# A graph, mixing and feed-forward block on one core: one reciprocal for two tiles, key sums between the qkv products, half of the weight splitting moved into layer 1

## Chip, cores, metric

The kernel runs on one core of one Trainium2 chip. The metric is the device time of one execution in microseconds. The engines are called as in the profile: PE (TensorE), DVE (the vector engine), ACT (ScalarE), POOL (GpSimd) and SP (SyncE, whose queue issues most of the transfers).

## What is computed

The reference, cut to what matters here (N = 3125 nodes, D = 256, 53125 edges with self loops and neighbours of a graph that `src` and `dst` give):

```python
xn = layernorm(x)
x  = x + gnn(xn, src, dst) + mix(xn)      # three graph layers: 256->1024->512->256
x  = x + ffn(layernorm(x))                # for the top 1561 rows by a router's score

# mix: per row, after a first scaling of xn
h   = relu(batchnorm(h @ w_qkv))                     # 768 wide: q, k, v parts
t   = proj(h);  s = proj(conv(t, w_dw, w_pw))        # second set of 768, in groups of 32
q, k, v of cat(t, s), 96 wide a group, norms clamped to a ball
vk  = v k^T over one position;  out = vk q / (sum(v) + eps)
ft  = proj(out) @ w_res + b_res;  fx = tanh(|ft|) ft / |ft|
```

With one position a row, the attention comes to `q * sum(k) * v / (v + eps)` in each group; the quotient is what the change is about. `eps` is scaled by the clamped norm of the row, so it is a tensor of its own (`veps`).

## The kernel before, in words

The work has these stages: norms, edge keys and the batch norm's statistics (up to 131 us); the mixing part (131 to 404 us); graph layer 1 (404 to 765 us), layers 2 and 3, the router's search, and the feed-forward part.

**Mixing part.** The 25 tiles of 125 rows are taken in NC = 5 chunks of 626 columns (features on the partitions). Every engine has its own loop over the chunks, and its order is written out by hand. All waits are on semaphores.

- PE (L2126 to L2158): `outs(c-1)` sums the squares of the previous chunk's four output tiles and multiplies the first two row tiles with `w_res`; `key_sums(c, n)` sums the keys within groups for each of the four tiles n (two of h, two of s) into banks 6 and 7; `outs_turned(c-1)` turns norms and does the other three row tiles; `hidden(c+1, m)` are the six qkv products of the next chunk, `spread(c+1)` its six convolution products, and `norm_spread(c+1)` broadcasts its norm sums, also into banks 6 and 7. `degrees` are in-degree counts from one-hot batches (chunks 0 and 1), `bias_product` (L1981) a product of `be1` with `w2` in chunk 2.
- DVE (L1088 to L1103): clamps the norms (`umax`, L1090), then for each tile `quotient` (L1032: an addition L1035, a reciprocal L1037, a product L1039) and `weigh` (L1042: the key product L1046 and the weighing L1048). `besides` puts one-hot batches (`half_batch`, L803), `scales`, pieces and rows between them. `rows_mixed` (L1051) reads the products with `w_res` of the previous chunk.
- ACT (L1618 to L1650): the square root that makes `veps` (L1620), evacuation and squares of the next chunk (`hidden`, `spread`), squares of the outputs (`out_square`), norms (`mixed_norms`), squares of weights, and the tables PREPARED_AT.

**Splitting for layer 1.** Layer 1's operands are float16 pairs of a high and a low part. There are twelve weight pieces (`wpieces`, L384: four of w1, eight of w2) and 25 row tiles. A piece is scaled by ACT into `wtemp` (`pieces_high`, L1517), its low part is made by DVE (`piece_low`, L1018), and ACT copies the high part back (`pieces_kept`, L1527). Rows go the same way (`rows_high`, L1532, `row_low`, L1024) through three buffers. PREPARED_AT and PIECES_AT / ROWS_AT (L445) say in which chunk, between which tiles, each is done.

**Layer 1.** For each tile PE adds up 25 count tiles times rows (`aggregate`, L2161), does half of the second product of tile t-2, turns the sums (`turn_y`), turns the normed rows of t-1 (`turn_x`), ends the second product and does the first product (`step1`, L2242). ACT begins a tile with `halve_rows` (L1680), DVE with `sum_rows` and ends it with `hidden1` (L1161). PE waits for all twelve pieces before tile 0:

```python
pe.wait_ge(sem("rows1_ready"), T)
pe.wait_ge(sem("ft_done"), T)
pe.wait_ge(sem("wpiece_done"), len(wpieces))
```

**Counts.** POOL scatters the edge counts into DRAM with 416 indirect transfers in 26 groups (L638), starting when edge indices and `evalue` (L1599) are ready, and sets a flag when a group has landed (`landing`, L632). SP fetches the counts of a tile into a ring of four; for layer 1 it waits for as many flags as the tile needs (`landed`, L514), and for the ring.

## Time and profile before

| | us |
|---|---|
| runs | 1365.85 median of 3 (1365.02 to 1368.14) |
| the profiled execution, own time | 1365.98 |
| its span in the profile | 1364.2 |
| PE busy | 1235.3 (91%) |
| DVE busy | 735.9 (54%) |
| ACT busy | 485.0 (36%) |
| POOL busy | 524.4 (38%) |
| mean granted clock of TensorE | 0.963 |

Shares of busy time are means over stages with different limits, so the stages have to be looked at one by one. Matmuls are all recorded at one helper's line (L1853); they are told apart by their tiles: `kones` are key sums, `ones` sums of squares, `wm` qkv, convolution or `w_res` products, `rows,scr` aggregations. A granted clock of 1.00 is 2.4 GHz, 0.50 is 1.2 GHz. "idle before" is the time that an engine had nothing to do just before an instruction, with what ended it.

### The profile page before, as it was taken

The numbers are of one execution on the slowest core, as the hardware profiler recorded it, in microseconds if no ns is written. First come the engines' busy times: TensorE is split into PE (matmuls) and PEld (weight loads), VectorE is DVE, ScalarE is ACT, GpSimd is POOL, SyncE is SP. The second block draws the span as 40 slices with busy tenths as digits, with TensorE's granted clock in tenths as the row PEclk, the third lists the DMA queues.
The fourth block names the chain that finished last, engine by engine and source line by source line (L and its number), as shares of the span: only waits on it lengthen the run. The fifth ranks groups of instructions, "written<-read, shape, count | busy, mean of one in ns | idle before, by whom it ended". The sixth has DMA issues, their size and how long they took to land.

```text
span 1364.2 us, 19298 instructions
## 1 busy us (share of the span) xinstructions
PE 1235.3 (91%) x6623; PEld 817.1 (60%) x6623; DVE 735.9 (54%) x1489; ACT 485.0 (36%) x1058; POOL 524.4 (38%) x551
## 2 busy tenths in 40 slices
PE   0998887897669999999999999999999999996995
PEld 0764564654445666666666566666666666663575
DVE  5674997868644555455454522322222268887244
ACT  2414674468532222232232223222122234432463
POOL 2001777777777777777701300070000000000623
PEclk9988898899879999999999999999999999998998
DMA  9880000000313222322122132212122146643201
GB/s 269 294 274 1 2 1 1 1 1 1 83 56 91 71 65 54 80 54 66 41 77 69 45 91 64 69 47 69 53 61 69 47 125 169 171 116 113 47 19 35
DMA packets 56391, 104.48 MB, mean 77 GB/s; under 512 B 25455, under 2 KB 40804, under 8 KB 56328
## 3 DMA queue, kind: packets, MB, share of 16 engines
q1 hardware_dynamic: 35800, 100.21, 25.9%
q0 software_dynamic: 20528, 3.47, 1.8%
q8 instruction: 35, 0.57, 0.2%
q14 instruction: 28, 0.23, 0.1%
HBM read 75.87 MB, written 27.67 MB: 76 GB/s over the span
## 4 chain that ended last, share of the span: by engine, by line
PE 80%; DVE 11%; ACT 4%; issue 2%; DMA 1%; SPq 0%; POOL 0%; DVEq 0%; ACTq 0%; POOLq 0%
PE psum L1853 77%; DVE scr L1037 3%; PE psum L2214 2%; DVE acc L807 1%; DMA rows<-in_x 1%; PE psum L2192 1%; DVE scr L1039 1%; DVE scr L1035 1%; DMA scr<-picked,eidx 0%; PE psum L1899 0%; PE psum L2207 0%; ACT scr L1566 0%; SPq L470 0%; DVE acc L809 0%; DVE scr L1320 0%
## 5 line engine op out<-in xcount | busy, mean ns | idle before, releaser
L642 POOL DMA_INDIRECT counts<-big,eidx x416 | 422.9, 1016 | 250.3 <-issue 130.8
L1853 PE MATMUL psum<-big,scr 125*125 125x512 f16 x1250 | 278.8, 379 | 1.0 <-DVE big L1157 1.0
L1853 PE MATMUL psum<-rows,scr 125*125 125x512 f16 x1250 | 274.7, 379 | 2.9 <-issue 1.6
L1853 PEld LDWEIGHTS psum<-rows,scr 125*125 125x125 f16 x1250 | 170.7, 137 | 102.3 <-issue 2.4
L1853 PEld LDWEIGHTS psum<-big,scr 125*125 125x125 f16 x1250 | 170.0, 137 | 94.9 <-DVE big L1157 1.5
L1853 PE MATMUL psum<-wb,scr 128*125 128x512 f16 x600 | 137.5, 379 | 1.4 <-DVE scr L1140 1.4
L1853 PEld LDWEIGHTS psum<-wb,scr 128*125 128x125 f16 x600 | 81.1, 137 | 45.8 <-DVE scr L1140 1.9
L1121 DVE TENSOR_SCALAR scr<-psum,col 125x256 f32<-125x256 f32 x25 | 12.1, 484 | 172.6 <-PE psum L1853 172.6
L1853 PE MATMUL psum<-big,wm 128*128 128x313 f32 x312 | 94.2, 453 | 8.2 <-ACT big L1556 4.6
L684 POOL DMA_INDIRECT scr<-picked,eidx x13 | 23.2, 1787 | 180.0 <-issue 180.0
L1853 PEld LDWEIGHTS psum<-big,wm 128*128 128x128 f32 x312 | 61.3, 201 | 38.7 <-issue 9.3
L1037 DVE RECIPROCAL scr<-scr 128x626 f32<-128x626 f32 x20 | 81.3, 4066 | 0.7
L1140 DVE TENSOR_TENSOR scr<-psum,scr 128x1000 f16<-128x1000 f32 x25 | 30.0, 1199 | 86.0 <-ACT scr L1697 86.0
L738 DVE BATCH_NORM_STATS2 col<-scr 125x6 f32<-125x512 f32 x75 | 49.5, 689 | 45.4 <-ACT scr L1706 28.1
L1853 PE MATMUL psum<-wa,scr 128*125 128x512 f16 x300 | 68.9, 380 | 1.0 <-DVE scr L1135 0.9
L673 POOL IOTA scr<- 125x63 f32 x1 | 0.2, 196 | 175.3 <-PE psum L1853 175.3
L1667 ACT ACTIVATE scr<-psum,col 128x125 f32<-128x125 f32 x100 | 37.3, 454 | 69.6 <-PE psum L2192 69.6
L1853 PEld LDWEIGHTS psum<-wa,scr 128*125 128x125 f16 x300 | 40.9, 137 | 24.8 <-DVE scr L1135 1.4
L664 POOL TENSOR_SCALAR scr<-wa,col 128x512 f32<-128x512 f32 x4 | 6.3, 1565 | 123.8 <-DVE col L1226 123.5
L1697 ACT CAST scr<-psum 128x1000 f16<-128x1000 f32 x25 | 24.8, 992 | 80.7 <-PE psum L1853 71.8
L807 DVE TENSOR_TENSOR acc<-acc,scr 104x2000 bf16<-104x2000 bf16 x32 | 38.2, 1194 | 19.7 <-PE psum L1853 19.5
L1853 PE MATMUL psum<-wc,scr 128*125 128x256 f32 x200 | 47.5, 380 | 1.2 <-ACT scr L1667 1.2
(388 smaller groups left out, 1805.8 us busy)
## 6 DMA issues: line engine op xcount, KB each, us to landing
scr<-counts SPq DMA_DIRECT2D x75, 683.6 KB
counts<-wb SPq DMA_DIRECT2D x25, 683.6 KB
counts<-big,eidx POOLq DMA_INDIRECT x416, 2.2
scr<-counts SPq DMA_DIRECT2D x75, 79.3 KB
scr<-in_x SPq DMA_DIRECT2D x25, 125.0 KB
picked<-big SPq DMA_DIRECT2D x5, 566.6 KB
rows<-in_x SPq DMA_DIRECT2D x5, 560.0 KB
out<-acc SPq DMA_DIRECT2D x5, 560.0 KB
```

The source lines that it names most:

```text
L642: pool.indirect_dma_start(cells, bass.IndirectOffsetOnAxis(ap=eidx[:, r * EQ + g:r * EQ + g + 1], axis=0), evalue[:, at_c:at_c + 1], None, ...
L684: pool.indirect_dma_start(got[:, g, :], None, picked_dram, bass.IndirectOffsetOnAxis(ap=picked[:, g:g + 1], axis=0), bounds_check=N - 1, o ...
L738: done.did(dve.bn_stats(st2[:, h, :], src[:, h * 512:(h + 1) * 512] if parts > 1 else src))
L807: done.did(dve.tensor_tensor(ohp, free(edp16, b * DB, [[2, DB // 2], [0, P], [1, 2]]), free(iop, 0, [[0, DB // 2], [2, P], [1, 2]]), ALU.i ...
L1035: done.did(dve.tensor_tensor(tdiv, v, veps, ALU.add))
L1037: done.did(dve.reciprocal(tdiv, tdiv))
L1039: done.did(dve.tensor_tensor(tdiv, tdiv, v, ALU.mult))
L1140: dve.tensor_tensor(xT16[:, 1].rearrange("p (b k) q -> p b (k q)", b=2), turned_halves(), xT16[:, 0].rearrange("p (b k) q -> p b (k q)", b ...
L1667: last = act.activation(xT[:, k, :], bank(5 + k // 4, 128, P, (k % 4) * P), ACT.Identity, scale=g[:, k:k + 1], bias=be[:, k:k + 1])
L1697: act.copy(xT16[:, 0].rearrange("p (b k) q -> p b (k q)", b=2), turned_halves()).then_inc(sem("xThi_done"), 1)
L1853: return pe.matmul(o, l, r, start=start, stop=stop)
L2214: last = pe.transpose(bank(5 + k // 4, 128, P, k % 4 * P), pre[0][:, k * 128:(k + 1) * 128], ident[:P, 0:P])
```

## The change

- DVE: `quotients` takes two tiles with one reciprocal: from one + eps and two + eps it makes their product's reciprocal, and multiplies each value with the other's sum first. The key product (`key`) is parted from `weigh`, and stands before the quotients or behind them. The second pair of tiles follows the same way.
- The clamped norm is made on ACT (`veps_made`: Relu of norm - 1, square root with a small bias, and a Relu for the row that is kept) right after the next chunk's evacuations; the norm sums go to banks 0 and 1 instead of 6 and 7. The maximum with 1 in `rows_mixed` becomes an addition of 1 inside the instruction.
- PE: each chunk begins with the first key sum, ahead of the output sums; the third and fourth key sums stand between the qkv products; `outs_turned` is parted, and its products come after the second key sum; in chunk 0 the norm sums come ahead of the turned edges. The bias product goes from chunk 2 to chunk 4.
- Layer 1 starts with four of twelve pieces (w1). The eight of w2 are split at its tiles 0 to 2, and PE waits for them before the first second product. They have buffers of their own, as many rows have.
- Rows are split later: nine by the end of chunk 3, fifteen in chunk 4, in more buffers, the last one as before.

```diff
-    PIECES_AT = {(2, 4): (0, 2), (2, 5): (2, 4), (3, 3): (4, 6), (3, 4): (6, 8), (3, 5): (8, 10), (4, 0): (10, 12)}
-    ROWS_AT = {(2, 4): (0, 3), (2, 5): (3, 6), (3, 3): (6, 9), (3, 4): (9, 12), (3, 5): (12, 15), (4, 3): (15, 18),
-               (4, 4): (18, 21), (4, 5): (21, 24)}
+    PIECES_AT = {(3, 1): (0, 2), (3, 4): (2, 4)}
+    ROWS_AT = {(3, 1): (0, 3), (3, 4): (3, 6), (4, 1): (6, 9), (4, 2): (9, 12), (4, 3): (12, 15), (4, 4): (15, 18),
+               (4, 5): (18, 24)}
...
-        def quotient(c, n):
-            src, half = part_of(c, n)
-            v = src[:, 4 + half, :]
-            done.did(dve.tensor_tensor(tdiv, v, veps, ALU.add))
+        def quotients(c, n):
...
+            done.did(dve.tensor_tensor(tdiv, one, veps, ALU.add))
+            done.did(dve.tensor_tensor(tdiv2, two, veps, ALU.add))
+            done.settle()
+            done.did(dve.tensor_tensor(one, one, tdiv2, ALU.mult))
+            done.did(dve.tensor_tensor(two, two, tdiv, ALU.mult))
+            done.did(dve.tensor_tensor(tdiv, tdiv, tdiv2, ALU.mult))
             done.settle()
             done.did(dve.reciprocal(tdiv, tdiv))
             done.settle()
-            done.did(dve.tensor_tensor(tdiv, tdiv, v, ALU.mult))
+            done.did(dve.tensor_tensor(one, one, tdiv, ALU.mult))
+            done.did(dve.tensor_tensor(two, two, tdiv, ALU.mult))
             done.settle()
...
         for c in range(NC):
-            dve.wait_ge(sem("norm_spread"), c + 1)
-            dve.tensor_scalar(halves(umax), pair(3), 1.0 / RMAX ** 2, 1.0, ALU.mult, ALU.max).then_inc(
-                sem("u_done"), 1)
             besides(c, 0)
+            key(c, 0)
             dve.wait_ge(sem("veps_done"), c + 1)
-            quotient(c, 0)
-            weigh(c, 0)
+            quotients(c, 0)
             besides(c, 1)
             if c >= 1:
                 rows_mixed(c - 1)
+            key(c, 1)
+            weigh(c, 0)
+            weigh(c, 1)
             besides(c, 2)
-            for n in range(1, 4):
-                quotient(c, n)
-                weigh(c, n)
-                besides(c, n + 2)
+            key(c, 2)
+            besides(c, 3)
+            quotients(c, 2)
+            besides(c, 4)
+            key(c, 3)
+            weigh(c, 2)
+            weigh(c, 3)
+            besides(c, 5)
...
         for t in range(HEAD):
             step1(t, t % 2, t % RING, 16 + t // RING * 16, min(t, 2))
+            if t < 2:
+                for c in range(W1_PIECES + 4 * t, W1_PIECES + 4 * t + 4):
+                    piece_low(c)
...
+        def veps_made(c):
+
+            act.wait_ge(sem("norm_spread"), c + 1)
+            act.wait_ge(sem("qk_done"), 4 * c)
+            act.activation(halves(veps), pair(0), ACT.Relu, scale=1.0 / RMAX ** 2, bias=minus_one).then_inc(
+                sem("u_done"), 1)
+            act.wait_ge(sem("u_done"), c + 1)
+            act.activation(veps, veps, ACT.Sqrt, scale=1e-30, bias=tiny).then_inc(sem("veps_done"), 1)
+            act.activation(halves(umax_row[c % 2]), pair(0, 1), ACT.Relu, scale=1.0 / RMAX ** 2,
+                           bias=minus_one[0:1]).then_inc(sem("row_kept"), 1)
...
+            for m in range(3):
+                hidden(c + 1, m)
             if c >= 1:
                 mixed_norms(c - 1)
+            out_square(c, 0)
             out_square(c, 1)
             besides(c, 1)
+            for m in range(3, NT):
+                hidden(c + 1, m)
+            for m in range(NT):
+                spread(c + 1, m)
+            norm_keep(c + 1)
+            veps_made(c + 1)
             out_square(c, 2)
...
             out_square(c, 3)
             besides(c, 3)
...
         act.wait_ge(sem("rows1_ready"), T)
         for t in range(HEAD):
+            if 1 <= t < 3:
+                pieces_kept(W1_PIECES + 4 * t - 4, W1_PIECES + 4 * t)
+            if t < 2:
+                pieces_high(W1_PIECES + 4 * t, W1_PIECES + 4 * t + 4)
             step1(t, t % 2, min(t, 2))
...
         for c in range(NC):
+            key_sums(c, 0)
             if c >= 1:
                 outs(c - 1)
-            key_sums(c, 0)
...
             key_sums(c, 1)
+            if c >= 1:
+                outs_rest(c - 1)
             degrees(c, 0)
...
+            if c == NC - 1:
+                key_sums(c, 2)
+                bias_product()
+                key_sums(c, 3)
+                break
+            for m in range(NT):
+                hidden(c + 1, m)
+                if m == (0 if c else 3):
+                    key_sums(c, 2)
+                if m == 4 and c >= 1:
+                    key_sums(c, 3)
+                for b in range(*BETWEEN.get((c, m), (0, 0))):
+                    degree(b)
+            if c == 0:
+                key_sums(c, 3)
...
-        pe.wait_ge(sem("wpiece_done"), len(wpieces))
+        pe.wait_ge(sem("wpiece_done"), W1_PIECES)
```

On ACT, chunk 2 ends with pieces 0 and 1 and rows 0 to 2; in chunk 3 the two are copied, pieces 2 and 3 and rows 3 to 5 are made between the third and the fourth evacuation, rows 6 to 8 at the end; in chunk 4 the other rows are made between the output root, the norms and the squares.

## Rows read from the trace of the kernel before

**Rows 1.** The page, part 4: shares of the chain that ended last, by line.
```profile
PE psum L1853 77%; DVE scr L1037 3%; PE psum L2214 2%; DVE acc L807 1%; DMA rows<-in_x 1%; PE psum L2192 1%; DVE scr L1039 1%; DVE scr L1035 1%; DMA scr<-picked,eidx 0%; PE psum L1899 0%; PE psum L2207 0%; ACT scr L1566 0%; SPq L470 0%; DVE acc L809 0%; DVE scr L1320 0%
```
**Rows 2.** Busy time by stage: span, then PE, PEld, DVE, ACT, POOL; clock, DMA.
```profile
131.50:178.60 47.10, 36.98 (x332) 22.46 (x333) 46.36 (x44) 30.19 (x55) 36.55 (x37) 0.86 0.02 2
178.60:235.10 56.50, 46.70 (x386) 31.00 (x378) 47.35 (x57) 34.78 (x77) 44.23 (x44) 0.94 0.02 1
235.10:294.20 59.10, 53.38 (x249) 33.69 (x238) 41.82 (x66) 32.91 (x64) 44.64 (x48) 0.91 0.02 1
294.20:349.00 54.80, 45.25 (x216) 28.82 (x218) 40.19 (x44) 39.48 (x76) 42.70 (x44) 0.94 0.02 1
349.00:388.10 39.10, 19.19 (x88) 13.30 (x87) 36.33 (x39) 16.52 (x41) 30.63 (x30) 0.72 0.42 110
403.70:439.40 35.70, 32.37 (x157) 20.67 (x158) 14.95 (x30) 10.71 (x18) 26.46 (x29) 1.00 0.39 99
439.40:765.00 325.60, 325.60 (x1622) 214.89 (x1621) 173.85 (x296) 87.99 (x135) 203.66 (x226) 1.00 0.24 60
```
**Rows 3.** TensorE in order of time, chunk 4: start, length, shapes, idle before.
```profile
369.56 2.45 PE L1853 MATMUL psum<-scr,kones 128*128 128x313 f32 x4 [6.28 <-DVE big L1046]
...
388.14 1.48 PE L1853 MATMUL psum<-big,ones 128*32 128x375 f32 x8 [7.64 <-ACT scr L1573]
```
**Rows 4.** TensorE's waits in chunk 3: total, times, longest.
```profile
PE psum L1853 <- ACT big L1556: 4.6, 1, 4.6
```
**Rows 5.** Vector engine by line, 131.5 to 388.1: busy and mean ns of one.
```profile
L1037 DVE RECIPROCAL scr<-scr 128x626 f32<-128x626 f32 x20 | 81.3, 4066 | 0.7
...
L1048 DVE TENSOR_TENSOR scr<-scr 128x626 f32<-128x626 f32 x14 | 11.4, 812 | 0.5
```
**Rows 6.** TensorE by line, the same stretch.
```profile
L1853 PE MATMUL psum<-wb,col 128*125 128x512 f32 x16 | 7.1, 599 | 0.0
```
**Rows 7.** ScalarE in order of time, chunk 3.
```profile
316.42 0.40 ACT L1592 ACTIVATE scr<-acc 125x256 f32<-125x256 f32 x1
...
319.22 0.71 ACT L1573 ACTIVATE scr<-scr 128x626 f32<-128x626 f32 x1
319.83 1.12 ACT L1530 COPY wb<-acc 128x512 f16<-128x512 f16 x2
320.86 1.33 ACT L1524 ACTIVATE acc<-wb,col 128x512 f16<-128x512 f32 x2
322.10 1.57 ACT L1537 ACTIVATE scr<-rows,col 125x256 f32<-125x256 f32 x3
323.70 1.02 ACT L1541 CAST rows<-scr 125x256 f16<-125x256 f32 x3
```
**Rows 8.** Both engines' and TensorE's own rows: weight pieces, then layer 1.
```profile
325.18 1.41 DVE L1021 SCALAR_TENSOR_TENSOR wb<-wb,col,acc 128x512 f16<-128x512 f32 x2
...
429.88 1.00 DVE L1172 TENSOR_SCALAR scr<-scr,col 125x1024 f32<-125x1024 f32 x1
...
420.14 0.47 ACT L1684 ACTIVATE scr<-psum,col 125x256 f32<-125x256 f32 x1 [1.13 <-PE psum L1853]
...
430.57 2.75 PE L1853 MATMUL psum<-wb,scr 128*125 128x512 f16 x12
```
**Rows 9.** Busy time and clock (the value before DMA) in short stretches.
```profile
174.00:176.00 2.00, 0.23 (x4) 0.00 (x0) 1.93 (x3) 0.69 (x2) 1.70 (x2) 1.00 0.02 0
260.00:262.00 2.00, 0.00 (x0) 0.00 (x0) 1.93 (x3) 1.73 (x7) 1.70 (x2) 0.69 0.01 0
262.00:264.00 2.00, 1.82 (x4) 1.27 (x5) 1.90 (x4) 1.28 (x4) 1.50 (x2) 0.50 0.06 8
```
**Rows 10.** The scatter's flag, the fetch that waits for it, the tile's first matmuls.
```profile
684.66 0.13 POOL L636 MEMSET col<- 125x1 f32 x1
...
684.98 0.86 SPq L470 DMA_DIRECT2D scr<-counts  x2
...
724.21 5.56 PE L1853 MATMUL psum<-rows,scr 125*125 125x512 f16 x25
```

More of the change, by code:

```diff
@@ L184, in _build @@
     sq3 = take("big", 3 * CW).rearrange("p (m c) -> p m c", m=3)
-    umax = take("big", CW)
+    tdiv2 = take("big", CW)
     h2in = big[:P, :].bitcast(F16).rearrange("p (t h d) -> p t h d", t=T, h=2)
@@ L444, in _build, with row_buffer, row_buffer_free, piece_buffer @@
                     ((22, 23), (23, 23), (23, 25), (25, 28), (28, 30), (30, 32)))
-    PIECES_AT = {(2, 4): (0, 2), (2, 5): (2, 4), (3, 3): (4, 6), (3, 4): (6, 8), (3, 5): (8, 10), (4, 0): (10, 12)}
-    ROWS_AT = {(2, 4): (0, 3), (2, 5): (3, 6), (3, 3): (6, 9), (3, 4): (9, 12), (3, 5): (12, 15), (4, 3): (15, 18),
-               (4, 4): (18, 21), (4, 5): (21, 24)}
+    PIECES_AT = {(3, 1): (0, 2), (3, 4): (2, 4)}
+    ROWS_AT = {(3, 1): (0, 3), (3, 4): (3, 6), (4, 1): (6, 9), (4, 2): (9, 12), (4, 3): (12, 15), (4, 4): (15, 18),
+               (4, 5): (18, 24)}
+    W1_PIECES = 4
+    LATE_ROWS = 9
+    sq_rows = free(sq3[:P], 0, [[D, 7], [1, D]])
+    def row_buffer(t):
+        if t < LATE_ROWS:
+            return xbuf[:, t % 3, :]
+        if 16 <= t < 19:
+            return xbuf[:, t - 16, :]
+        return sq_rows[:, t - 9 if t < 16 else t - 19, :]
+    def row_buffer_free(t):
+        if t < LATE_ROWS:
+            return max(t - 2, 0)
+        if t < 16:
+            return 0
+        return t - 9
+    def piece_buffer(c):
+        if c < W1_PIECES:
+            return wtemp[c % 2]
+        o = 2 * NC * CW + (c - W1_PIECES) * 256
+        return big[:, o:o + 256].bitcast(F16)
     def piece_scale(c):
@@ L1020, in piece_low @@
             dve.wait_ge(sem("wpiece_high"), c + 1)
-            dve.scalar_tensor_tensor(out=kept[:, 0, :], in0=raw, scalar=piece_scale(c), in1=wtemp[c % 2],
+            dve.scalar_tensor_tensor(out=kept[:, 0, :], in0=raw, scalar=piece_scale(c), in1=piece_buffer(c),
                                      op0=ALU.mult, op1=ALU.subtract).then_inc(sem("wpiece_low"), 1)
@@ L1030, in part_of @@
             return (hTs[c % 2], n) if n < 2 else (sTs[c % 2], n - 2)
-        def quotient(c, n):
-            src, half = part_of(c, n)
-            v = src[:, 4 + half, :]
-            done.did(dve.tensor_tensor(tdiv, v, veps, ALU.add))
+        def quotients(c, n):
+            sides = []
+            for k in (n, n + 1):
+                src, half = part_of(c, k)
+                sides.append(src[:, 4 + half, :])
+            one, two = sides
+            done.did(dve.tensor_tensor(tdiv, one, veps, ALU.add))
[4 more added lines that the diff above has]
+            done.did(dve.tensor_tensor(tdiv, tdiv, tdiv2, ALU.mult))
             done.settle()
@@ L1080, in besides @@
                 scales()
-            if c == 3 and at == 0:
+            if c == 4 and at == 4:
                 read_be2w()
@@ L2034, in hidden, with spread @@
                 norm_pair(c, m // 2 - 1)
-        def spread(c):
+        def spread(c, lo=0, hi=NT):
             hT = hTs[c % 2]
-            for m in range(NT):
+            for m in range(lo, hi):
                 if m < 2:
@@ L2056, in key_sums @@
             pe.wait_ge(sem("qk_done"), c * 4 + n)
-            if n == 0:
-                pe.wait_ge(sem("u_done"), c + 1)
+            if c == 0 and n == 0:
+                pe.wait_ge(milestone("needs_ready"), AFTER["needs_ready"])
+                pe.wait_ge(milestone("value_kept"), AFTER["value_kept"])
             if n >= 2:
@@ L2085, in outs, with outs_rest @@
             for j in range(2):
+                res(c, j)
+        def outs_rest(c):
+            for j in range(2, G):
+                if j == 4 and c == 0:
+                    pe.wait_ge(sem("degree_kept"), 1)
+                if j == 4 and c == 1:
+                    pe.wait_ge(milestone("dinv_read"), AFTER["dinv_read"])
+                    pe.wait_ge(milestone("bounds_read"), AFTER["bounds_read"])
+                if j == 4 and c == NC - 1:
+                    pe.wait_ge(milestone("be2w_read"), AFTER["be2w_read"])
                 res(c, j)
@@ L2095, in outs_turned @@
             last.then_inc(sem("out_turned"), 1)
-            for j in range(2, G):
-                if j == 4 and c == 0:
-                    pe.wait_ge(sem("degree_kept"), 1)
-                if j == 4 and c == 1:
-                    pe.wait_ge(milestone("dinv_read"), AFTER["dinv_read"])
-                    pe.wait_ge(milestone("bounds_read"), AFTER["bounds_read"])
-                if j == 4 and c == 2:
-                    pe.wait_ge(milestone("be2w_read"), AFTER["be2w_read"])
-                res(c, j)
         def degrees(c, at):
@@ L2120, in _ @@
         norm_pair(0, 5)
+        norm_spread(0)
         turn_edges("index", 6, bwd)
@@ L2232, in product2 @@
             if lo == 0:
+                if isinstance(t, int) and t == 0:
+                    pe.wait_ge(sem("wpiece_done"), len(wpieces))
                 pe.wait_ge(sem("xT2_done"), t + 1)
```

127 lines of the change are left out of this document (63 added, 64 removed).

## The prediction, made before the change was run

> **What bounds the kernel now.** I read the chain that ended last first. TensorE carries nearly all of it, and the one other big item is the vector engine's reciprocal at L1037 [rows 1]. So the question is where vector work stands in TensorE's way. I then cut the span into stages, each of the first four ending where TensorE starts the output sums of a chunk [rows 2]. The mixing part runs from 131.5 to 403.7 us. In chunk 0 the vector engine is busy for 46.4 of 47.1 us, in chunk 4 for 36.3 of 39.1. In chunks 1 to 3 TensorE is busy for 46.7 of 56.5, 53.4 of 59.1 and 45.3 of 54.8 us. From 439.4 to 765.0 TensorE is busy all the time: a microsecond lost there cannot be hidden, one lost before it is lost for good, and one won in the mixing part is kept only if nothing takes it back. Third, the waits: in chunk 4 TensorE waits some 6 us for each key product and 7.6 us for the last square [rows 3]; in chunk 3 it waits for ScalarE instead, 4.6 us in one piece [rows 4].
>
> **Shared reciprocals.** Of each chunk's four tiles the change divides two at a time. Before, a tile costs an addition, a reciprocal, a product with it, the key product and the weighing: 4.1 + 4 x 0.84 = 7.5 us, 30 us a chunk, and 0.8 us for the clamped maximum, which moves to ScalarE [rows 5]. After, a pair costs two additions, three products, one reciprocal and two products: 4.1 + 7 x 0.78 = 9.5 us (instructions that need not wait for one another start 0.73 us apart, dependent ones 0.84), and four key products and weighings of 0.85 us each make 6.8. That is 26 us a chunk, 4.8 less. It counts only where the vector engine bounds.
>
> **Chunk by chunk.** I lay out the new order with these durations and the busy times of the stages [rows 2].
> - Chunk 0 is still bound by the vector engine. It starts 2 us later than now (the key sum comes first, behind four more instructions), needs 26 us and ten half batches of 1.42 us ((46.4 - 30.8) / 11 by its busy time [rows 2]), and ends near 174; with the last batch and one key sum TensorE starts the output sums at 175.8, not 178.6. Won: 2.8.
> - Chunk 1: the vector engine has 26 + 14.2 + 3.2 = 43.4 us, TensorE 46.7. Key sums now stand between the qkv products and the reciprocals run under them, so TensorE's own 46.7 are what is left, and 0.8 of waiting: 47.5 instead of 56.5. Won: 9.0.
> - Chunk 2: the bias product (7.1 us [rows 6]) leaves for chunk 4. Of 53.4 busy us 46.3 stay, less 2 that came from the slow clock after a gap. A new wait of 2.1 us comes in: the output sums need all four squares, and ScalarE makes the last two only after the three new instructions for the clamped norms (2.0 us; behind them queue the squares, for which only the output sums wait). 46.4 instead of 59.1; as parts of it overlap I take 46.1. Won: 13.0.
> - Chunk 3: 45.3 busy, some 3 of them from the slow clock, plus the 2.1. Between the third and the fourth qkv evacuation ScalarE now has five norms (3.0, they begin at 316.42 and the next work at 319.22), two squares (1.3), two copies of weight pieces, two new pieces and three rows (1.1 + 1.3 + 2.6): 9.3 us [rows 7], while TensorE has 4.6 of other work. It waits about 5, and restarts slow for 2. Sum 51.6 instead of 54.8. Won: 3.2.
> - Chunk 4: bound by the vector engine. Key sum 1.2, then 26, the mixed rows 2.4, the bias 0.8, twelve rows of 0.37 (4.4) and 1.7 of waiting for TensorE's products make 36.5 from the norm sums on; from output sums to output sums 34.0 instead of 39.1. The bias product lies under the second pair's reciprocal; without that cover it would cost its 7.1. Won: 5.1.
> - The 15.6 us from the last output sums to layer 1 stay. The six rows and the last one that are now split behind the last weighing (2.6 us) lie under it.
> Sum of the mixing part: 33.1 us won. Bounds: 24, if each of chunks 1 to 3 keeps another 3 us of waits; 42, if ScalarE delays nothing in chunk 3 and the busy times shrink to what they are at full clock.
>
> **Second weight in layer 1.** Eight of twelve pieces move from a place where they hid to the first tiles of layer 1, where TensorE has nearly no gap. At tile 0 ScalarE makes four high parts (4 x 0.65 [rows 7]), 2.1 of them in a gap: 0.45 us late. After tile 0 the vector engine makes four low parts (2.7), ScalarE copies them (the last one 0.5 later) and makes four more high parts (2.6) before it may read tile 1's sums, which it read at 420.14, right behind tile 0: 6.2 us, and TensorE has nothing in its queue that could go ahead. At tile 1 the vector engine ended at 430.9 and TensorE began the second product at 430.57; both now come 6.2 + 2.5 (slow clock, below) later, but the product has to wait for four more low parts and the last copy, 3.3 more [rows 8]. So 12 us lost in all; later tiles run as before. About 2.5 of the 12 are clock: the clock stayed at 1.00 (2.4 GHz) over two microseconds in which TensorE had 0.2 us of work, but after a stretch that left 260 to 262 us wholly empty it was 0.50 (1.2 GHz) [rows 9], and the gap here is over 6. The Trainium skill, in "TensorE: Matmul & The Clock Gate", section "What's actually happening", puts it the other way round: the slow level is the default and activity lifts it. By it the moved pieces are worse than their own length; taken without any clock effect the loss would be some 9.5, and the sum 2.5 lower. The rows of this trace agree with it. Bounds of this term: 8 (the clock holds and the copies overlap better) and 15 (a second slow restart at tile 2).
>
> **More row buffers, key sums moved past queues, three more instructions on ScalarE:** they are in the sums above, or cost nothing while ScalarE is busy for 30 to 40 us of a 46 us chunk. GpSimd's scatter of the counts starts 3 to 4 us later, since the edge values are copied behind the clamped norms; at first nobody waits for it. SyncE's queue gets no new work.
>
> **Sum.** 33.1 - 12 = 21.1 us off the profiled execution's 1365.98 (span 1364.2): 1344.9. The median, 1365.85, is 0.13 from it, so I say 1345.
>
> **Rivals.**
> (a) The scatter becomes the bound. Tile 23 of layer 1 may be fetched only when a flag is set, at 684.66; the fetch goes out at 684.98, takes some 7 us with the next one behind it, and TensorE starts that tile at 724.21 [rows 10]. With a scatter 4 us later the earliest start is about 696, so no more than 28.5 us can be won, whatever the mixing part gives. If layer 1's loss is 8 and the mixing part wins 37 or more, the result is 1365.98 - 28.5 = 1337.5, with TensorE waiting once near the end of layer 1. For it: the fetches of tiles 22 and 23 already wait now. Against: it needs both good bounds. Chance 0.17.
> (b) The waits change places. The mixing part wins only some 22 because TensorE waits in every chunk for squares and ScalarE's queue; with 12 lost: 1356. For it: chunk 3 shows that ScalarE's order can stop TensorE. Chance 0.17.
> (c) Slower. The key sum of the third tile now stands in TensorE's queue between the qkv products, and waits for the second key product; that one stands behind the mixed rows, which stand behind the first pair's reciprocal. In my layout the products and this wait end within 1.5 us of each other. If the reciprocal starts late by d, TensorE, and everything behind it in its queue, loses d in three and a half chunks; above d = (33.1 - 12) / 3.5 = 6 us the whole is slower. A full pair behind (9.5 us) gives 1345 + 33 = 1378. Against it: what starts the pair, the clamped norm, is ready 2 us into the chunk. Chance 0.06.
> (d) The change does not do what it says: what it takes from the vector engine is hidden anyway in the middle chunks and layer 1 takes back the rest, 13 against 12: 1365. The waits in chunk 4 speak against it [rows 3]. Chance 0.04.
>
> **How the numbers follow.** Forecast 0.56, (a) 0.17, (b) 0.17, (c) 0.06, (d) 0.04. The range reaches to the low case less 2.5 us for the scatter's own uncertainty, 1335, and to (b) plus 1, 1357 (24 won and 15 lost is 1357 as well). About 0.2% (2.7 us) is what a measurement of this kernel can tell from no change. Faster takes the forecast, (a), (b) and a little of (d): 0.90; same 0.03; slower 0.07.
>
> **What would show it.** Right: two reciprocals a chunk; chunks 1, 2, 3 of about 47, 46 and 52 us from output sums to output sums; layer 1's first aggregation 33 us earlier; a gap of 6 us on TensorE before tile 1's turned sums and of 3 before tile 2's second product; then TensorE without a gap. Wrong: chunks 1 to 3 longer than 50 with TensorE waiting for key products or squares; a wait on SyncE for the flags that reaches TensorE at tile 23; or ScalarE and the vector engine overlapping the pieces so that layer 1 loses less than 8.

## The result, and the profile after

The changed kernel takes 1360.1 us (median of six runs, 1357.4 to 1362.8), the kernel before beside it 1365.9: a ratio of 0.9951 (95% interval 0.9940 to 0.9962). It is faster, but by 5.8 us, not by 21; 1360.1 lies 3 us outside the range. The profiled execution took 1359.73 us (span 1357.9), the mean granted clock was 0.968 instead of 0.963. TensorE is busy for 91% of the span, the vector engine for 52% (709.9 us), ScalarE for 36%, GpSimd for 39%.

The chain that ended last, by line, answers to [rows 1]: the reciprocal, now L1075, went from 3% to 1%. The one-hot batches (L836) still stand in the chain.

```profile
PE psum L1928 80%; PE psum L2303 2%; DMA rows<-in_x 1%; DVE acc L836 1%; PE psum L2281 1%; DVE scr L1075 1%; SPq L497 1%; DMA scr<-picked,eidx 0%; PE psum L2296 0%; PE psum L1974 0%; ACT scr L1645 0%; DVE wb L1050 0%; ACT scr L1619 0%; ACT scr L1811 0%; ACT scr L1626 0%
```

The stages after, cut at the same places as [rows 2] (length, then PE, PEld, DVE, ACT, POOL with counts; clock, DMA share, GB/s). The first begins at the first key sum.

```profile
131.76:179.21 47.45, 39.95 (x337) 23.40 (x337) 42.63 (x49) 30.70 (x56) 37.47 (x31) 0.86 0.02 2
179.21:231.35 52.14, 47.63 (x373) 30.32 (x372) 41.30 (x57) 35.60 (x78) 41.51 (x40) 0.96 0.02 1
231.35:279.42 48.07, 43.78 (x216) 28.39 (x216) 34.22 (x61) 25.33 (x48) 37.56 (x38) 0.96 0.02 1
279.42:333.63 54.21, 45.13 (x212) 28.81 (x212) 32.13 (x42) 33.31 (x63) 41.24 (x41) 0.91 0.02 1
333.63:368.45 34.82, 24.13 (x100) 15.15 (x100) 30.57 (x44) 22.77 (x56) 27.73 (x27) 0.89 0.42 111
384.25:432.94 48.69, 36.27 (x158) 22.89 (x159) 19.96 (x38) 20.29 (x34) 37.33 (x41) 0.89 0.28 73
432.94:755.00 322.06, 322.06 (x1604) 212.25 (x1603) 169.71 (x294) 87.98 (x135) 217.17 (x241) 1.00 0.24 61
```

Set against the ends of the stages before, the mixing part reads so:

| stage | won, forecast | won, measured |
|---|---|---|
| chunk 0 (ends 179.2; was 178.6) | 2.8 | -0.6 |
| chunk 1 (52.1; was 56.5) | 9.0 | 4.4 |
| chunk 2 (48.1; was 59.1) | 13.0 | 11.0 |
| chunk 3 (54.2; was 54.8) | 3.2 | 0.6 |
| chunk 4 (34.8; was 39.1) | 5.1 | 4.3 |
| last output sums to first aggregation (15.8) | 0 | -0.2 |
| three tiles of layer 1 (48.7; was 35.7) | -12 | -13.0 |
| sum, at the fourth aggregation | 21.1 | 6.5 |

From the fourth aggregation to 755 us (765 before) TensorE is busy all the time in both kernels, and 6.3 us is the difference of the two profiled executions. So 13.6 of the 14.6 us that are missing lie in the mixing part, which won 19.5 us instead of 33.1. Layer 1 lost 13.0 us where 12 were forecast.

The length of a stage differs by up to 1.5 us between traces: chunk 2 takes 48.07 us here, and 46.52 and 46.61 us in the traces of e2 and e4 below, whose edits do not touch it.

The places where TensorE stood still, in order of time (start, length, engine, line, shapes, idle before). No vector instruction of the key product is left among the long ones. Instead there are the batches (174.83), the last square behind ScalarE's new work (279.42; the same 2.56 stands at 333.63), ScalarE's pieces of chunk 3 (312.80), the end of chunk 4, and the weight pieces in layer 1 (407.57, 422.38).

```profile
174.83 0.61 PE L1928 MATMUL psum<-acc 104*32 104x125 bf16 x16 [3.44 <-DVE acc L838]
...
176.82 2.46 PE L1928 MATMUL psum<-scr,kones 128*128 128x313 f32 x4
...
279.42 1.48 PE L1928 MATMUL psum<-big,ones 128*32 128x375 f32 x8 [2.56 <-ACT scr L1626]
...
312.80 4.22 PE L1928 MATMUL psum<-big,wm 128*128 128x313 f32 x8 [5.17 <-ACT big L1609]
...
368.45 1.48 PE L1928 MATMUL psum<-big,ones 128*32 128x375 f32 x8 [9.39 <-ACT scr L1626]
...
407.57 0.68 PE L2296 MATMUL psum<-ident,scr 125*128 125x125 f32 x2 [6.65 <-DVE scr L1178]
408.04 1.87 PE L2303 MATMUL psum<-ident,scr 125*128 125x125 f32 x8
409.71 3.96 PE L1928 MATMUL psum<-wa,scr 128*125 128x512 f16 x12
...
422.38 4.47 PE L1928 MATMUL psum<-wb,scr 128*125 128x512 f16 x12 [3.31 <-ACT wb L1583]
```

Why the batches were late is on the vector engine. It had run ahead of TensorE and was itself waiting for TensorE to free a one-hot buffer: 2.48 us at 154.08 in chunk 0, and in chunk 1

```profile
225.38 1.20 DVE L836 TENSOR_TENSOR acc<-acc,scr 104x2000 bf16<-104x2000 bf16 x1 [6.42 <-PE psum L1928]
```

TensorE frees that buffer only with the products of a batch, which its written-out order places late, behind other work. These waits come to 9.3 us in chunks 0 and 1. They are not new: the kernel before had 6.7 us of them (L807, the longest 5.6), and without the sharing (e14) they are 7.1. So only some 2 us of the time won by the shared reciprocals turned into this wait. The forecast had no term for it.

### The profile page after: what moved, and what is told of

The parts are those of the page before. It is cut to its first block, busy times and chain, and to the rows that moved or that the text cites. A ratio compares the mean times of both kernels' runs of the same rounds, so it can differ in the third digit from the quotient of the medians.

```text
span 1357.9 us, 19319 instructions
## 1 busy us (share of the span) xinstructions
PE 1237.4 (91%) x6623; PEld 815.1 (60%) x6623; DVE 709.9 (52%) x1504; ACT 489.9 (36%) x1063; POOL 534.6 (39%) x553
## 4 chain that ended last, share of the span: by engine, by line
PE 83%; DVE 7%; ACT 5%; issue 2%; DMA 1%; SPq 1%; POOL 0%; ACTq 0%; DVEq 0%; POOLq 0%
PE psum L1928 80%; PE psum L2303 2%; DMA rows<-in_x 1%; DVE acc L836 1%; PE psum L2281 1%; DVE scr L1075 1%; SPq L497 1%; DMA scr<-picked,eidx 0%; PE psum L2296 0%; PE psum L1974 0%; ACT scr L1645 0%; DVE wb L1050 0%; ACT scr L1619 0%; ACT scr L1811 0%; ACT scr L1626 0%
## 5 line engine op out<-in xcount | busy, mean ns | idle before, releaser
L671 POOL DMA_INDIRECT counts<-big,eidx x416 | 433.2, 1041 | 251.8 <-issue 127.9
L836 DVE TENSOR_TENSOR acc<-acc,scr 104x2000 bf16<-104x2000 bf16 x32 | 38.2, 1194 | 22.2 <-PE psum L1928 22.0
L1928 PE MATMUL psum<-wc,scr 128*125 128x256 f32 x200 | 47.5, 380 | 1.2 <-ACT scr L1738 1.2
L1749 ACT CAST rows<-scr 125x256 f32 (+1 forms) x25 | 10.1, 404 | 95.4 <-DVE scr L1169 95.4
```

The lines of the kernel that those rows point to most:

```text
L671: pool.indirect_dma_start(cells, bass.IndirectOffsetOnAxis(ap=eidx[:, r * EQ + g:r * EQ + g + 1], axis=0), evalue[:, at_c:at_c + 1], None, ...
L836: done.did(dve.tensor_tensor(ohp, free(edp16, b * DB, [[2, DB // 2], [0, P], [1, 2]]), free(iop, 0, [[0, DB // 2], [2, P], [1, 2]]), ALU.i ...
L1928: return pe.matmul(o, l, r, start=start, stop=stop)
```

## The experiments

Each is an edit of the changed kernel. Times are medians, ratios stand against the kernel before on the same chip (1366 to 1367 us), and the change alone is 0.9951, 1360.1 us. Four edits first, each to one of the waits above.

**Weight pieces inside the tiles (e1).** The pieces are made between a tile's turned rows and its hidden rows, on both engines, instead of between the tiles.

```diff
-            if 1 <= t < 3:
-                pieces_kept(W1_PIECES + 4 * t - 4, W1_PIECES + 4 * t)
-            if t < 2:
-                pieces_high(W1_PIECES + 4 * t, W1_PIECES + 4 * t + 4)
-            step1(t, t % 2, min(t, 2))
+            step1(t, t % 2, min(t, 2), (W1_PIECES + 4 * t, W1_PIECES + 4 * t + 4) if t < 2 else None)
```

> The changed kernel, but in layer 1 the eight pieces of the second weight are made inside tiles 0 and 1: on ScalarE high parts and copies behind the turned rows and ahead of the relu, on the vector engine low parts ahead of the first layer's sum. Theory 1 (the loss of 13 us in layer 1 is a matter of place: the pieces stand in front of what TensorE waits for, and there are gaps of 4.7 us on ScalarE and 2.9 us on the vector engine behind it): from the first aggregation to the fourth 36 to 38 us instead of 48.7 (35.7 before the change), the kernel 11 to 13 us shorter than the changed one, about 18 below the kernel before. Rival (the work itself is too much there; whatever its place TensorE waits for it or for what it delays): 44 us or more for the same stretch, at most 5 us won.

1345.0 us, ratio 0.9837 (0.9819 to 0.9856): 15.1 us. The three tiles take 35.66 us, to the hundredth what they took before the change, and the clock stays at 1.00. The stage and TensorE's rows of tile 1:

```profile
382.58:418.24 35.66, 32.38 (x157) 20.56 (x158) 19.81 (x38) 19.61 (x34) 27.48 (x29) 1.00 0.40 99
```
```profile
400.02 0.43 PE L2295 MATMUL psum<-ident,scr 125*128 125x125 f32 x2 [1.08 <-DVE scr L1178]
400.29 1.02 PE L2302 MATMUL psum<-ident,scr 125*128 125x125 f32 x8
401.36 2.80 PE L1927 MATMUL psum<-wa,scr 128*125 128x512 f16 x12
```

So the 13 us were the price of the place, not of the work: the wait is 1.08 instead of 6.65 us, and 1.02 and 2.80 us stand where the change took 1.87 and 3.96 at the slow clock. Tile 2 had the same trouble: its first product took 4.47 us behind the wait of 3.31, and takes 2.75 here without one. The start of this run was 1.7 us earlier, which is most of the other 2.

**One-hot buffers freed earlier (e2).** TensorE takes the products of two batches earlier in its order.

```diff
-        BETWEEN = {(0, 5): HALF_BATCHES[0][2], (1, 1): (23, 25), (1, 2): (25, 26), (1, 3): (26, 27), (1, 4): (27, 28)}
+        BETWEEN = {(0, 4): HALF_BATCHES[0][2], (1, 1): (23, 25), (1, 2): (25, 26), (1, 3): (26, 27), (1, 4): (27, 28)}
...
-            spread(c + 1, 3, NT)
+            spread(c + 1, 3, 5)
+            if c == 1:
+                degrees(c, 4)
+            spread(c + 1, 5, NT)
...
-            degrees(c, 4)
+            if c != 1:
+                degrees(c, 4)
```

> The changed kernel, but TensorE uses two pairs of one-hot batches earlier: batches 12 and 13 behind the fifth qkv product of chunk 0 instead of the sixth, batches 28 and 29 between the convolution products of chunk 1 instead of behind the norm sums. Theory 1 (the vector engine's waits of 2.5 us in chunk 0 and 6.4 us in chunk 1 are waits for a free one-hot buffer, and TensorE then waits for the batches): both waits go, the output sums of chunk 1 (now 231.35) start 6 to 8 us earlier, the kernel is 6 to 8 us shorter. Rival (chunks 0 and 1 are bound by the amount of work on the two engines, the waits are only where the slack shows): at most 2 us won.

1354.5 us, ratio 0.9913 (0.9894 to 0.9932): 5.6 us, just under what was expected. The vector engine's wait in chunk 0 is gone and that of 6.42 us is 1.28. TensorE's longest wait for a batch in chunk 0 is 2.53 instead of 3.44. From the first key sum to the output sums chunk 0 takes 44.15 us instead of 47.45; the forecast had 44.3. In chunk 1 the batch waits are gone, but only 0.9 us is won, since the square is now late there too:

```profile
224.80 1.47 PE L1928 MATMUL psum<-scr,ones 128*32 128x375 f32 x16 [1.75 <-ACT scr L1626]
```

**Squares ahead of the clamped norms (e3).** ScalarE makes the last two squares between the evacuations.

```diff
             for m in range(NT):
                 spread(c + 1, m)
+                if c >= 1 and m in (3, 4):
+                    out_square(c, m - 1)
             norm_keep(c + 1)
             veps_made(c + 1)
-            out_square(c, 2)
-            out_square(c, 3)
+            if c == 0:
+                out_square(c, 2)
+            if c == 0:
+                out_square(c, 3)
```

> The changed kernel, but in chunks 1 to 3 ScalarE makes the third and fourth squares of the outputs between the evacuations of the convolution products, not behind the three instructions for the clamped norms. Theory 1 (output sums wait 2.6 us in chunks 3 and 4 for squares that queue behind the norms, and the gap slows the clock at the start of chunk 4): both waits shrink under 0.5 us, 5 to 7 us won. Rival (the squares then delay the norm sums by their own 1.3 us, and the key product becomes the wait): 2 us or less.

1355.5 us, ratio 0.9916 (0.9899 to 0.9932): 4.6 us. The waits of 2.56 us are gone; the norm pairs wait 1.42 instead of 0.81 in three chunks, 1.8 us in all, about what is missing to the 5 to 7 expected:

```profile
275.54 0.46 PE L1932 MATMUL psum<-big,ones 128*32 128x313 f32 x2 [1.42 <-ACT scr L1602]
...
279.12 0.84 PE L1932 MATMUL psum<-big,ones 128*32 128x375 f32 x8
```

**ScalarE's pieces of chunk 3 a step earlier (e4).**

```diff
-            if (c, at) == (3, 1):
+            if (c, at) == (3, 0):
```

> The changed kernel, but in chunk 3 ScalarE copies two pieces and makes two pieces and three rows ahead of the first qkv evacuation, not between the third and the fourth. Theory 1 (TensorE's 5.2 us wait in chunk 3 is this work in ScalarE's queue): the wait and the slow restart behind it go, chunk 3 takes 47 to 48 us from output sums to output sums instead of 54.2, 6 to 7 us won. Rival (the work only moves its wait to the first evacuation, since it waits for low parts from the vector engine): 2 us or less.

1350.9 us, ratio 0.9891 (0.9872 to 0.9910): 9.2 us, of which chunk 3 alone is 6.4:

```profile
277.90:325.75 47.85, 43.56 (x211) 28.62 (x211) 32.16 (x42) 33.30 (x63) 36.53 (x36) 0.96 0.02 1
```

ScalarE does the same 33.3 us of work in it; only its order differs. The wait of 5.17 us came from the place in ScalarE's queue alone. Of the other 2.8 us, 1.5 lie in chunk 2 and 1.0 between the last output sums and layer 1, which the edit does not touch.

**Runs on chips that hold the kernel up.** The next four ran on a chip on which the kernel before takes 1904.6 us.

> The change with each tile taking its own reciprocal again (two of one tile's width for a pair instead of one of twice the width: 4.07 us once becomes about 3.1 us twice at the durations of the kernel before), in the same place and order. Theory 1, VectorE's time counts wherever VectorE's list ends last: about 2 us a pair and 4.2 us a chunk of added VectorE work; chunks 0, 4 and partly 1 pass it on, chunks 2 and 3 (bounded by TensorE and by ScalarE's pieces) hide most: slower than the change by 8 to 10 us, 1368 to 1370. Rival, the order of the work alone is what the change won in the mixing part and the reciprocals lie beside TensorE: slower by 3 us or less, 1360 to 1363.

> The change with all four of the earlier edits together (pieces of layer 1's second half made inside tiles 0 and 1, the freed one-hot buffers, squares before the clamped norms, ScalarE's pieces of chunk 3 a step earlier). Alone they gained 15.1, 5.6, 4.6 and 9.2 us, 34.5 in sum. Theory 1, they lie in stretches of their own and add: 1326 to 1330. Rival, the scatter on GpSimd and its flags become the bound once TensorE reaches them about 28 us earlier than in the kernel before: TensorE waits for a transfer of the sparse part around row tile 22, and the time stops near 1337. Second rival, the waits overlap (each gain includes the same jitter of the start and the same queue): 1338 to 1344 with no wait at the sparse part.

> All four edits, and the edge values are copied ahead of the spread norms, so that GpSimd's scatter starts about 3 to 4 us earlier. If the scatter's flags bind in the run of all four edits, this is 3 to 4 us faster than it. If they don't, it is the same within 1 us.

> The change with the bias product (one instruction of 7.1 us on TensorE) back in chunk 2. Theory 1, chunk 2 is bounded by TensorE and the product lies in a wait in chunk 4: chunk 2 longer by 6 to 7 us, chunk 4 no shorter, 1366 to 1367. Rival, chunk 2 has room for it or chunk 4 gets shorter by as much: 0 to 2 us slower, 1360 to 1362.

They took 1899.3, 1839.1, 1830.9 and 1881.4 us. None of the questions can be read from them, since the extra time lies on the stretch that the edits are about: in e5 TensorE is busy for 70 of the 500 us between 200 and 700 us. In this stretch, while GpSimd issues the scatter, the other engines get through few instructions, and what they wait for is not in the profile; behind the scatter, from 712 to 760 us, TensorE is busy for 39.6 of 48 us again. In the fourth run of the bias product's edit TensorE's batch products come one every 2.80 us instead of sixteen in 0.42:

```profile
230.42 0.26 PE L1928 MATMUL psum<-acc 104*32 104x125 bf16 x1 [2.54 <-issue]
233.22 0.26 PE L1928 MATMUL psum<-acc 104*32 104x125 bf16 x1 [2.54 <-issue]
```

The same held for a repetition of e5 (e11, 1900.5 us) and three of e8 (e12, e15 and e16: 1866.0, 1871.7 and 1877.8 us, with the same expectation) on three chips in all. So what moving the bias product was worth stays open. The change's own trace shows its place: at 350.97, between the two key sums of chunk 4, for 7.03 us, ahead of a wait of 9.39 us. The key sum behind it ends at 359.05, and the vector engine takes it up at 365.27 without a wait. So in chunk 4 nothing waits for it; what chunk 2 won by its leaving is not shown.

**All four edits together (e9).**

> The change with all four of the earlier edits together, once more, since on the chip of the first try every kernel, the one before too, was held up for some 500 us while GpSimd's scatter ran. Alone they gained 15.1, 5.6, 4.6 and 9.2 us, 34.5 in sum. Theory 1, they lie in stretches of their own and add: 1326 to 1330. Rival, the scatter on GpSimd and its flags become the bound: TensorE waits for a transfer of the sparse part around row tile 22, and the time stops near 1337. Second rival, the gains overlap: 1338 to 1344 with no wait at the sparse part.

1347.9 us, ratio 0.9867 (0.9850 to 0.9885): 12 us under the change, where the four alone sum to 34.5. The mixing part did add up: the last output sums start at 348.63 instead of 368.45, the fourth aggregation at 400.24 instead of 432.94. The rest was given back near the end of layer 1. These are the aggregations of row tiles 20 to 24, and GpSimd's flags (its memsets):

```profile
642.32 5.56 PE L1931 MATMUL psum<-rows,scr 125*125 125x512 f16 x25
...
660.33 8.23 PE L1931 MATMUL psum<-rows,scr 125*125 125x512 f16 x25 [3.60 <-DMA scr<-counts]
...
680.96 5.61 PE L1931 MATMUL psum<-rows,scr 125*125 125x512 f16 x25 [3.55 <-DMA scr<-counts]
...
701.86 7.96 PE L1931 MATMUL psum<-rows,scr 125*125 125x512 f16 x25 [6.45 <-DMA scr<-counts]
...
718.50 5.56 PE L1931 MATMUL psum<-rows,scr 125*125 125x512 f16 x25
```
```profile
675.25 0.12 POOL L665 MEMSET col<- 125x1 f32 x1
...
695.88 0.13 POOL L665 MEMSET col<- 125x1 f32 x1
...
697.11 0.10 POOL L665 MEMSET col<- 125x1 f32 x1 [1.10 <-DMA counts<-big,eidx]
```

This is rival (a) of the forecast, reached: three waits of 13.6 us in all, and two slow restarts of 2.7 and 2.4 us (8.23 and 7.96 for 5.56). A tile comes 6.0 us behind its flag (695.88 to 701.86).

**The edge values first as well (e10).** GpSimd starts 1.8 us earlier.

```diff
-        veps_made(0)
         act.wait_ge(milestone("value_turned"), AFTER["value_turned"])
         act.copy(evalue, bank(7, 128, EQ * ER)).then_inc(milestone("value_kept"), 1)
+        veps_made(0)
...
         norm_pair(0, 5)
-        norm_spread(0)
         turn_edges("index", 6, bwd)
         turn_edges("value", 7, fwd)
+        norm_spread(0)
```

> All four edits, and the edge values copied ahead of the spread norms, once more, beside the run above. If the scatter's flags bind in the run of all four edits, this is 3 to 4 us faster than it. If they don't, it is the same within 1 us.

1345.7 us, ratio 0.9847 (0.9831 to 0.9863): 2.2 us under e9, between the two expectations, and the intervals overlap. In the trace the scatter starts at 129.2 instead of 131.0 and ends at 695.0 instead of 694.9. So an earlier start did not bring an earlier end. The run reads this only roughly, since the edit also made the mixing part 3.7 us longer (222.2 instead of 218.5 us from the first key sum to the last output sums).

**Flags raised earlier (e13).** The edit is on top of the four. A flag was raised after all 16 issues of the next group; now it is raised after 4 of them.

```diff
-            if n >= 1:
-                landing(n - 1)
+                if n >= 1 and r == n * ROWS_A_GROUP:
+                    landing(n - 1)
```

> The change with all four edits, and each flag of the scatter raised after the first 4 of the next group's 16 transfers instead of after all 16. Theory, in the run of all four edits TensorE waits for flags and not for the scatter itself: a flag comes a whole group (16 issues of about 1.29 us) after its group was issued, so 12 issues earlier are about 15 us at row tile 23; the last tile then needs the flag at 697 us and starts about 6 us behind it, at 703 instead of 718.5: 1331 to 1335. Rival, the transfers themselves land late or the loads behind the flags collide: no more than 4 us faster than all four edits, 1344 to 1348.

1334.0 us, ratio 0.9750 (0.9737 to 0.9764), as expected and 14 us under e9. One wait of 3.45 us is left, at row tile 23, with a slow restart. The last tile starts 6.2 us behind the last flag:

```profile
688.69 8.63 PE L1931 MATMUL psum<-rows,scr 125*125 125x512 f16 x25 [3.45 <-DMA scr<-counts]
...
706.13 5.61 PE L1931 MATMUL psum<-rows,scr 125*125 125x512 f16 x25
```
```profile
683.09 0.13 POOL L665 MEMSET col<- 125x1 f32 x1
...
699.90 0.10 POOL L665 MEMSET col<- 125x1 f32 x1 [1.22 <-DMA counts<-big,eidx]
```

**Reciprocals not shared (e14).** Same order, same place, two reciprocals for a pair.

```diff
             done.settle()
-            done.did(dve.tensor_tensor(one, one, tdiv2, ALU.mult))
-            done.did(dve.tensor_tensor(two, two, tdiv, ALU.mult))
-            done.did(dve.tensor_tensor(tdiv, tdiv, tdiv2, ALU.mult))
-            done.settle()
             done.did(dve.reciprocal(tdiv, tdiv))
+            done.did(dve.reciprocal(tdiv2, tdiv2))
             done.settle()
             done.did(dve.tensor_tensor(one, one, tdiv, ALU.mult))
-            done.did(dve.tensor_tensor(two, two, tdiv, ALU.mult))
+            done.did(dve.tensor_tensor(two, two, tdiv2, ALU.mult))
```

> The change with each tile taking its own reciprocal again, a third try on a chip without the long hold-up. Theory 1: VectorE's added time (one reciprocal of 4.07 us more, one multiplication of 0.8 us less for each of two pairs a chunk) is passed on by chunks 0, 4 and partly 1: slower than the change by 8 to 12 us, 1368 to 1372. Rival, the order of the work alone is what the change won in the mixing part: slower by 3 us or less, 1360 to 1363.

1362.7 us, ratio 0.9970 (0.9959 to 0.9981): 2.6 us slower than the change, whose interval just touches this one. That is the time of the rival, not of theory 1. The expectation of e5 had put an unshared reciprocal at 3.1 us; in this trace one takes 4.0 to 4.1. Its stages:

```profile
130.53:181.22 50.69, 41.96 (x337) 24.56 (x337) 46.04 (x45) 30.81 (x56) 39.91 (x35) 0.80 0.02 2
181.22:232.46 51.24, 46.03 (x373) 29.67 (x372) 44.64 (x53) 35.59 (x78) 40.20 (x40) 1.00 0.02 2
232.46:280.01 47.55, 42.46 (x217) 27.92 (x216) 37.33 (x57) 25.33 (x48) 36.80 (x39) 1.00 0.02 1
280.01:334.76 54.75, 45.67 (x212) 29.16 (x212) 35.43 (x38) 33.31 (x63) 41.48 (x44) 0.91 0.02 1
334.76:371.33 36.57, 24.16 (x99) 15.35 (x99) 33.94 (x40) 22.86 (x56) 28.18 (x29) 0.83 0.43 109
```

From the first key sum to the last output sums that is 240.8 us; the change takes 236.7. So sharing is worth 4.1 us in these two traces and 2.6 by the medians: 3.2 in chunk 0, 1.7 in chunk 4, and in the three chunks between nothing that can be read (0.9 us the other way). The vector engine has 16.5 us more work in these stages (197.4 for 180.9 us), and 12.4 of it fill time in which it stood idle in the change, mostly waiting for TensorE. Sharing is also worth less than half a reciprocal: a pair takes 9.5 us shared (134.50 to 143.98) and 11.2 us unshared (133.72 to 144.89), since three multiplications of 0.8 us come in for one reciprocal of 4.07.

**The best version without sharing (e17).** e13 with the edit of e14.

> All four edits and the early flags, with each tile taking its own reciprocal. Theory: the three multiplications that a shared reciprocal adds slow GpSimd's scatter beside them (its 416 issues took 554.2 us from first to last in the change with reciprocals of their own, 555.6 before, and 562.8 to 567.7 in the nine traces with shared ones), while the sharing won 4 us of VectorE's time in the mixing part. So the scatter ends near 686, no flag is waited for, and the time is TensorE's alone: 1330 to 1333, a little faster than with shared reciprocals (1334.0). Rival: the scatter's length has another cause, it stays at 565 us, and the mixing part's 4 us are lost or lie under the same flag: 1334 to 1338 with a wait for the counts at row tile 23.

1339.5 us, ratio 0.9799 (0.9781 to 0.9817): slower than e13 by 5.5 us. Half of the theory held: TensorE waits for no flag, and the scatter is 7 us shorter. The other half, 4 us for the sharing, was wrong here. The last output sums start at 364.91 instead of 350.22, 13.0 of these 14.7 us in the chunks themselves (the start of the run is 1.7 later). The whole loses less than that because e13 gives 6.5 us back at row tile 23: the wait of 3.45, and 8.63 us for what takes 5.56. With the waits of the four edits gone, the vector engine's time counts in chunk after chunk: TensorE waits 2.6 us in chunk 3 for the mixed rows and 2.9 in chunk 4 for a key product. The same cut of work was worth 4 us behind other waits and 13 us without them.

The scatter's length in the four traces (issues of L671: shortest, median, longest in ns; first and last start), in this order: the change, e13, e14, e17.

```profile
L671 POOL DMA_INDIRECT counts<-big,eidx x416: 966/972/2253, 132.6 to 695.4; - x139
```
```profile
L671 POOL DMA_INDIRECT counts<-big,eidx x416: 966/972/2259, 132.0 to 697.7; - x139
```
```profile
L671 POOL DMA_INDIRECT counts<-big,eidx x416: 965/972/1886, 131.4 to 685.6; - x139
```
```profile
L671 POOL DMA_INDIRECT counts<-big,eidx x416: 966/972/2255, 133.6 to 692.3; - x139
```

## Why the prediction was right in direction and wrong in size

Of the 14.6 us missing, 3.4 lie in chunk 0, 4.6 in chunk 1, 2.0 in chunk 2, 2.6 in chunk 3, and 2.0 in all the rest.

- **Layer 1: right but for one restart.** 12 us forecast, 13.0 measured, with the two gaps where they were said to be (6.65 before tile 1's turned sums for "over 6", 3.31 before tile 2's product for 3) and the slow restart. Behind tile 1's gap the clock cost 2.0 us (1.87 and 3.96 us against 1.02 and 2.80 in e1), 2.5 forecast. But there was a second slow restart, at tile 2 (4.47 us for 2.75), 1.7 us more, which the forecast had only in its upper bound. The Trainium skill, in "TensorE: Matmul & The Clock Gate", section "What's actually happening", says that activity lifts a throttled default; the slow matmuls right behind the gap agree. What the forecast didn't say is that the loss was avoidable: e1 takes it away entirely.
- **Chunk 0: the step that failed first.** "Needs 26 us and ten half batches ... Won: 2.8." It laid out the vector engine as if nothing stopped it, though the trace before had 6.7 us of waits for one-hot buffers. The engine waited 2.48 us for a one-hot buffer, and the last batches came late for TensorE, which stood for 3.44 us and restarted slow. With the buffers freed (e2) the stage takes 44.15 us; the forecast was 44.3.
- **Chunk 1: the same step.** "TensorE's own 46.7 are what is left, and 0.8 of waiting." TensorE was busy for 47.6 us, but stood still for 4.5: 1.47 and 1.02 us for batches whose buffer the vector engine had waited 6.42 us for, 0.67 for the mixed rows and 1.35 for ScalarE's norms. TensorE's own time is what is left only if every other queue arrives in time. Freed buffers alone bring 0.9 us here, since the square is late next. In e13, which has the four edits, the chunk takes 49.4 us and not the 47.5 forecast: TensorE is busy for 47.5 and stands for 1.9, 1.2 of them for ScalarE's norms.
- **Chunk 2: mechanism right, size under.** Busy 43.8 us, forecast 44.3. The wait for the squares was forecast at 2.1 us and was 2.56; other waits of 1.7 us, 1.35 of them for ScalarE's norms, were left out. 48.1 us instead of 46.1.
- **Chunk 3: the waits right, the clock wrong.** TensorE stood still for 9.1 us, 5.17 of them in the forecast's wait of "about 5"; forecast were 2.1 + 5 and 2 for a slow restart (with the 42.3 us of work that makes 51.4, not the 51.6 it says). But "45.3 busy, some 3 of them from the slow clock" took those 3 us away, and TensorE was busy for 45.1 again, since each new wait brought its own slow start (4.22 us at 312.80 for what takes 2.38 elsewhere). e4 shows that 6.4 us of the chunk were ScalarE's order alone.
- **Chunk 4 and the tail: right within 1 us.** The bias product hid.
- **Shared reciprocals: the place right, the credit too large.** The forecast took 4.8 us a chunk off the vector engine and let it count in chunks 0 and 4, for which it said 2.8 + 5.1. e14 shows 3.2 and 1.7 us for the sharing there. So of the 19.5 us of the mixing part some 4 are the sharing. The other 15 are the rest of the change together: the new order, the norms on ScalarE, the bias product, and the pieces moved to layer 1. No run takes these apart.
- **Rival (b) is nearest to what happened:** the waits change places and the mixing part wins only some 22, priced at 1356. It won 19.5. The forecast's own sign for it showed: chunks 1 and 3 took over 50 us, with TensorE waiting for squares in chunk 3. But (b) names squares and ScalarE's queue, and in chunks 0 and 1, with 8.0 of the 14.6 us missing, TensorE's largest waits were for one-hot batches. The squares, ScalarE's pieces and the one-hot buffers each put something that TensorE needs behind something that it doesn't. The forecast had the first two waits nearly right (2.1 for 2.56, about 5 for 5.17) and the third not at all.
- **Rival (a)** did not bind in the change (TensorE never waited for the counts), but does 12 us below it. It was put too far away: the cap was said to be 28.5 us under the kernel before, from a scatter that starts 4 us later and keeps its length. e9 stopped at 19. The start was right (132.60 for 128.09), the length wasn't: 562.8 us instead of 555.6.

## What to carry to other kernels

When work is taken off one engine, its queue can run ahead to the next limit (a buffer that another engine's written-out order frees late), so look for waits of that kind in the trace before, and lay out all queues to that limit before crediting busy time as won. Where a new instruction goes in an in-order queue decides more than what it costs: here 13 us (e1) and 6 us (e4) went away by moving the same work by one step. A gain read beside other waits can be far too low (4 us, then 13 with these gone), and the flag of a slow producer is worth a look before its pace is.

## What the runs showed of the hardware

**GpSimd's issues are slowed by the kind of vector work beside them, not by its amount.** An issue takes 0.97 us while the vector engine runs a reciprocal, and 1.26 to 1.53 beside multiplications of two tiles in SBUF. The change's trace, GpSimd and then the vector engine (start, length):

```profile
135.45 1.42 POOL L671 DMA_INDIRECT counts<-big,eidx  x1 [0.31 <-issue]
137.17 1.26 POOL L671 DMA_INDIRECT counts<-big,eidx  x1 [0.30 <-issue]
138.73 0.97 POOL L671 DMA_INDIRECT counts<-big,eidx  x1 [0.30 <-issue]
...
141.29 0.97 POOL L671 DMA_INDIRECT counts<-big,eidx  x1 [0.30 <-issue]
142.56 1.53 POOL L671 DMA_INDIRECT counts<-big,eidx  x1 [0.30 <-issue]
```
```profile
136.78 0.80 DVE L1072 TENSOR_TENSOR big<-big,scr 128x626 f32<-128x626 f32 x1
137.50 0.81 DVE L1073 TENSOR_TENSOR scr<-scr,big 128x626 f32<-128x626 f32 x1
138.34 4.07 DVE L1075 RECIPROCAL scr<-scr 128x626 f32<-128x626 f32 x1
142.44 0.81 DVE L1077 TENSOR_TENSOR big<-big,scr 128x626 f32<-128x626 f32 x1
```

Counted over this whole trace, an overlap of 0.15 us or more taken as beside: of 62 issues beside only such instructions, with both inputs in SBUF, 50 took over 1.1 us; none did of the 29 beside a reciprocal alone, nor of the 45 beside key products and others that read one input from PSUM. The vector engine is less busy than before in the mixing part, and yet the scatter is 7 us longer (562.8 for 555.6 us from first issue to last). With unshared reciprocals it takes 554.2 us again, and in e17 558.7 where e13 has 565.7. The Trainium skill says it in "GPSIMD Engine Reference", section "8. Key points": GpSimd shares its SBUF interfaces with the vector engine and contends with vector instructions that have two SBUF inputs. These rows agree. By that rule the trade of one reciprocal for three products was never free for the scatter, and the prediction did not weigh it.

**Some chips hold every engine up while the scatter runs.** On three of the five chips of the experiments the kernel before took 1904 to 1905 us instead of 1366, in every run. In e5 TensorE's clock was 0.51 between 200 and 700 us, where it was nearly idle. The scatter itself took 580.1 us (132.1 to 712.2), 26 us more than in e14, the same kernel on another chip. What makes these chips differ, no run here shows.
